# Second attention of a two-layer block: scores per pair of heads, first as rows for the maximum, then with keys on the partitions

## The reference, cut to what matters

```python
q = (x @ Wq).reshape(b, t, 32, 16).transpose(0, 2, 1, 3)
k = (x @ Wk).reshape(b, t, 8, 16).transpose(0, 2, 1, 3)
v = (x @ Wv).reshape(b, t, 8, 16).transpose(0, 2, 1, 3)
q = _apply_rope(q, cos, sin)
k = _apply_rope(k, cos, sin)
k_h = jnp.repeat(k, 4, axis=1)
v_h = jnp.repeat(v, 4, axis=1)
scores = jnp.einsum('bhqd,bhkd->bhqk', q, k_h) / math.sqrt(16)
scores = jnp.where(causal[None, None], jnp.finfo(scores.dtype).min, scores)
attn = jax.nn.softmax(scores, axis=-1)
ctx = jnp.einsum('bhqk,bhkd->bhqd', attn, v_h)
```

## Time and profile before

| | before |
|---|---|
| Three runs, median (lowest to highest) | 1173.53 us (1171.95 to 1173.54) |
| The profiled execution: its own time | 1172.01 us |
| Its span in the trace | 1170.4 us |
| Loop of the second attention, first transposes to last exponentials | 907.6 to 1085.2 us |
| One unit of it (four heads) | 11.03 us |

### The profile page before, as it was taken

How to read it: one execution, slowest core, us unless ns; L and a number is a source line. 1 busy time by engine, 2 the same in 40 slices (tenths; PEclk the granted TensorE clock), 3 DMA queues, 4 the chain that set the end, 5 groups by cost and what they waited for, 6 DMA issues and landing times. The chain is left out here.

```text
span 1170.4 us, 19511 instructions
## 1 busy us (share of the span) xinstructions
PE 1135.4 (97%) x6634; PEld 953.0 (81%) x6634; DVE 787.2 (67%) x2463; ACT 705.8 (60%) x1646; POOL 410.8 (35%) x342
## 2 busy tenths in 40 slices
PE   7999999999999999999999999999999899999997
PEld 5888888888888888888888778888888677777786
DVE  6767776766776777767677752222336899999775
ACT  6656665656765666665665644453112899999524
POOL 4654554354544445544452513334013210020200
PEclk9999999999999999999999999999999999999999
DMA  6011111111110111100100012222001223321001
GB/s 231 19 39 42 39 28 28 28 35 38 46 28 19 37 37 37 36 28 19 37 19 28 1 46 72 63 80 74 1 18 29 56 67 81 99 50 34 1 1 72
DMA packets 30346, 51.04 MB, mean 44 GB/s; under 512 B 5680, under 2 KB 6576, under 8 KB 30256
## 3 DMA queue, kind: packets, MB, share of 16 engines
q1 hardware_dynamic: 29680, 48.85, 14.7%
q10 hardware_dynamic: 576, 1.05, 0.2%
HBM read 38.35 MB, written 2.10 MB: 35 GB/s over the span
## 5 line engine op out<-in xcount | busy, mean ns | idle before, releaser
L491 POOL TENSOR_TENSOR turned<-turned,sin 128x512 f32<-128x512 f32 x73 | 94.6, 1296 | 276.3 <-ACT turned L347 276.3
L363 ACT ACTIVATE probs<-probs,neg_max 128x256 f32<-128x256 f32 (+1 forms) x256 | 119.7, 473 | 11.3 <-DVE neg_max L591 11.3
L1488 ACT ACTIVATE a_probs<-a_probs,a_neg_max 128x512 f32<-128x512 f32 (+3 forms) x256 | 122.6, 562 | 0.1
L1672 DVE CUSTOM_DVE_ANT_0 a_probs<-bank,a_mask 128x512 f32<-128x512 f32 (+3 forms) x256 | 109.8, 485 | 6.0 <-PE bank L1892 6.0
L494 POOL TENSOR_TENSOR turned<-turned,by_cos 128x512 f32<-128x512 f32 x73 | 101.2, 1386 | 11.1 <-DVE by_cos L564 5.7
L96 PE MATMUL bank<-wo_hi,oT_hi 128*128 128x512 f32 x256 | 100.3, 392 | 1.7 <-DVE oT_lo L654 1.7
L745 PE MATMUL bank<-xT_hi,wq_hi 128*128 128x512 f32 x256 | 101.4, 396 | 0.0
L745 PE MATMUL bank<-xT_lo,wq_hi 128*128 128x512 f32 x256 | 100.2, 392 | 0.0
L745 PE MATMUL bank<-xT_hi,wq_lo 128*128 128x512 f32 x256 | 100.1, 391 | 0.0
L96 PE MATMUL bank<-wo_hi,oT_lo 128*128 128x512 f32 x256 | 99.9, 390 | 0.0
L96 PE MATMUL bank<-wo_lo,oT_hi 128*128 128x512 f32 x256 | 99.7, 389 | 0.0
(11 more groups left out here) (234 smaller groups left out, 3155.4 us busy)
## 6 DMA issues: line engine op xcount, KB each, us to landing
staged<-weights SPq DMA_DIRECT2D x70, 256.0 KB, 2.7
f_staged<-weights_f SPq DMA_DIRECT2D x33, 256.0 KB, 2.7
a_q_stack<-a_qT_hi SPq DMA_DIRECT2D x64, 64.0 KB, 2.0
rows<-x_rows SPq DMA_DIRECT2D x2, 1024.0 KB, 7.2
a_k_stack<-a_kT_hi SPq DMA_DIRECT2D x64, 32.0 KB, 2.0
a_q_stack<-a_qT_lo SPq DMA_DIRECT2D x32, 64.0 KB, 2.0
out<-rows SPq DMA_DIRECT2D x8, 256.0 KB, 2.0
a_raw<-weights_qkv SPq DMA_DIRECT2D x4, 384.0 KB, 4.8
```

Source lines behind the costliest of these rows:

```text
L363: act.activation(probs[:, s % 2, h, 0:width], probs[:, s % 2, h, 0:width], ACT.Exp, bias=neg_max[:, s % 2, h:h + 1], scale=SCALE0, accum_o ...
L491: pool.tensor_tensor(at, at, sin[:, :], ALU.mult).then_inc(sin_done, 1)
L1488: act.activation(row_probs(s, qt), row_probs(s, qt), ACT.Exp, bias=neg_max[:, h, qt:qt + 1], scale=-1.0).then_inc(exp_done, 1)
L1672: dve.tensor_tensor_reduce(row_probs(s, qt), ps_s[bank][:, at:at + seen], mask[:, SEQ - seen:SEQ], -SCALE1, HIGHEST, ALU.add, ALU.min, neg ...
```

## The change

The heads are now taken in pairs `p`, 32 of them. For each head the scores are made twice. First as before, queries on the partitions: `scores(p, step)` has three steps, and in each a bf16 matmul of the identity with a causal mask goes ahead of the score matmuls, which add to it. `find_maxima(p, step)` on DVE reduces both heads of the pair in one instruction straight from PSUM and writes only the maxima. `turn_maxima(p)` on PE transposes the eight columns of maxima, `read_maxima(p)` on ACT copies them to SBUF as rows, and `load_maxima(p)` on SP moves them with eight transfers of one row into row 48 of the pair's query stack. `key_scores(p, step)` then makes the scores a second time with the keys on the partitions; key row 48 holds -1, so the maximum is subtracted in the contraction. `exps(p, step)` on ACT reads both heads from PSUM and writes the probabilities in the layout that `apply` wants, so that `turn` and `copy_turned` fall away. `keep_causal(p, step)` on POOL sets the probabilities above the diagonal of the four diagonal blocks to zero. `apply` has three steps, each behind POOL's `kept`.

A stack holds one head with 48 rows, once at partition 0 and once at partition 64 for the pair's other head. `load_stacks(u)` makes 18 transfers of 16 rows, in three buffers; the first three units are loaded ahead of the loop. Scores and key scores share three pairs of banks; the unit's output has one bank in place of two. POOL also sets two pads and two bf16 constants ahead of the loop, and SP loads six rows of -1.

The core of the diff (names and constants that changed alone, and the removed functions, which the listing above shows, are left out):

```diff
-            def load_keys(u, version, arrived):
+            def load_keys(u, arrived):
                 b, g = divmod(u, KV1)
-                for part, source in enumerate((kT_hi, kT_lo, kT_hi)):
-                    to = part * PAIR_ROWS + version * HD1
-                    sp.dma_start(k_stack[to:to + HD1, u % 2, version, :].bitcast(F32),
-                                 source[g * HD1:(g + 1) * HD1, b * SEQ:(b + 1) * SEQ].bitcast(F32)).then_inc(arrived, 16)
+                for at in (0, HALF_ROWS):
+                    for part, source in enumerate((kT_hi, kT_lo, kT_hi)):
+                        to = at + part * HD1
+                        sp.dma_start(k_stack[to:to + HD1, u % BUFFERS, :].bitcast(F32),
+                                     source[g * HD1:(g + 1) * HD1, b * SEQ:(b + 1) * SEQ].bitcast(F32)).then_inc(arrived, 16)
 
             def load_queries(u, pair, arrived):
                 b, g = divmod(u, KV1)
-                first = (g % 2) * GROUP_COLS + pair * PAIR_ROWS
-                for part, source in enumerate((qT_hi, qT_hi, qT_lo)):
-                    sp.dma_start(q_stack[part * PAIR_ROWS:(part + 1) * PAIR_ROWS, u % 2, pair, :].bitcast(F32),
-                                 source[first:first + PAIR_ROWS, g // 2, b * SEQ:(b + 1) * SEQ].bitcast(F32)).then_inc(arrived, 16)
+                for n, at in enumerate((0, HALF_ROWS)):
+                    first = (g % 2) * GROUP_COLS + (2 * pair + n) * HD1
+                    for part, source in enumerate((qT_hi, qT_hi, qT_lo)):
+                        to = at + part * HD1
+                        sp.dma_start(q_stack[to:to + HD1, u % BUFFERS, pair, :].bitcast(F32),
+                                     source[first:first + HD1, g // 2, b * SEQ:(b + 1) * SEQ].bitcast(F32)).then_inc(arrived, 16)
 
             def load_stacks(u):
-                for n in range(2):
-                    arrived = first_stack_in if u == 0 and n == 0 else stack_in[u % 2]
-                    load_keys(u, n, arrived)
-                    load_queries(u, n, arrived)
+                first = first_stack_in if u == 0 else stack_in[u % BUFFERS]
+                load_keys(u, first)
+                load_queries(u, 0, first)
+                load_queries(u, 1, stack_in[u % BUFFERS])
+
+            def load_maxima(p):
+
+                u, pair = divmod(p, 2)
+                sp.wait_ge(max_read, p + 1)
+                for n, at in enumerate((0, HALF_ROWS)):
+                    for qt in range(SEQ_TILES):
+                        row = n * SEQ_TILES + qt
+                        sp.dma_start(q_stack[at + STACK:at + STACK + 1, u % BUFFERS, pair, qt * P:(qt + 1) * P].bitcast(F32),
+                                     max_rows[row:row + 1, p % 2, :].bitcast(F32)).then_inc(max_in[p % 2], 16)
...
+            for n in range(BUFFERS):
+                for at in (0, HALF_ROWS):
+                    sp.dma_start(k_stack[at + STACK:at + STACK + 1, n, :].bitcast(F32), minus[0:1, :]).then_inc(minus_in, 16)
             sp.wait_ge(part_lo, TURNS_OF[0])
...
+            for u in range(BUFFERS):
                 load_stacks(u)
-                if u == 3:
+            for p in range(PAIRS1):
+                load_maxima(p)
+                u = p // 2
+                if p % 2 == 1 and u >= 1 and u + 2 < UNITS1:
+                    if u + 2 == KV1:
+                        sp.wait_ge(part_lo, TURNS_OF[1])
+                    sp.wait_ge(keys_scored, STEPS * (p - 1))
+                    load_stacks(u + 2)
...
+            def read_maxima(p):
+                act.wait_ge(max_turned, p + 1)
+                if p >= 2:
+                    act.wait_ge(max_in[p % 2], MAX_DMAS * (p // 2))
+                act.activation(max_rows[0:2 * SEQ_TILES, p % 2, :], ps_m[0:2 * SEQ_TILES, 0:P], ACT.Copy).then_inc(max_read, 1)
+
+            def exps(p, step):
+
+                act.wait_ge(keys_scored, STEPS * p + step + 1)
+                if step == 0 and p >= RING_PAIRS:
+                    act.wait_ge(applied, STEPS * ((p - RING_PAIRS) // 2 + 1))
+                width, at = STEP_WIDTH[step], step * SEQ
+                act.activation(pair_probs(p)[:, :, at:at + width], ps_pair[KEY_BANKS[step]][:, :, 0:width], ACT.Exp,
+                               scale=SCALE1).then_inc(exp_done, 1)
 
...
+            def keep_causal(p, step):
+
+                pool.wait_ge(exp_done, STEPS * p + step + 1)
+                for kb in KEY_STEPS[step]:
+                    at = step * SEQ + TURNED_AT[kb]
+                    probs = pair_probs(p)[:, :, at:at + P]
+                    last_kept = pool.affine_select(probs, probs, [[0, 2], [1, P]], ALU.is_ge, nothing, base=0,
+                                                   channel_multiplier=-1)
+                last_kept.then_inc(kept, 1)
+
...
+            def find_maxima(p, step):
+
+                if step == 0 and p >= 2:
+                    dve.wait_ge(max_turned, p - 1)
+                by_tile = maxima[:, p % 2, 0:2 * SEQ_TILES].rearrange("p (h t) -> p h t", t=SEQ_TILES)
+                dve.wait_ge(scored, STEPS * p + step + 1)
+                for qt in SCORE_STEPS[step]:
+                    at = SCORES_AT[qt]
+                    found = dve.tensor_reduce(by_tile[:, :, qt:qt + 1], ps_pair[SCORE_BANKS[step]][:, :, at:at + (qt + 1) * P],
+                                              mybir.AxisListType.X, ALU.max)
+                found.then_inc(max_done, 1)
...
+            def scores(p, step):
+
...
+                    elif pair == 0:
+                        pe.wait_ge(stack_in[u % BUFFERS], stacks_loaded(u))
+                if p == 0 and step == 1:
+                    pe.wait_ge(part_lo, PARTS_AFTER[TILES - 2][0] + 1)
+                elif p == 0 and step == 2:
+                    pe.wait_ge(sin_done, 4 * (TILES - 1))
+                elif step == 2 and p >= AHEAD1:
+                    pe.wait_ge(exp_done, STEPS * (p - AHEAD1) + 1)
+                elif p >= AHEAD1 + 1:
+                    pe.wait_ge(exp_done, STEPS * (p - AHEAD1 - 1) + step + 2)
+                elif p >= 1:
+                    pe.wait_ge(max_done, STEPS * (p - 1) + step + 1)
+                banks = ps_pair[SCORE_BANKS[step]]
+                first, end = CAUSAL_AT[step]
+                for n in range(2):
+                    pe.matmul(banks[:, n, first:end], ident_b[:, :], causal_b[:, 0:end - first], start=True, stop=False,
+                              skip_group_check=True)
+                for qt in SCORE_STEPS[step]:
+                    for n, rows_at in enumerate((0, HALF_ROWS)):
+                        part = slice(rows_at, rows_at + STACK)
+                        mm = pe.matmul(banks[:, n, SCORES_AT[qt]:SCORES_AT[qt] + (qt + 1) * P],
+                                       q_stack[part, u % BUFFERS, pair, qt * P:(qt + 1) * P],
+                                       k_stack[part, u % BUFFERS, 0:(qt + 1) * P], start=False, stop=True,
                                        skip_group_check=True)
-                    mm.then_inc(scored, 1)
...
+            def turn_maxima(p):
+                pe.wait_ge(max_done, STEPS * (p + 1))
+                if p == 0:
+                    pe.wait_ge(sin_done, 4 * TILES)
+                else:
+                    pe.wait_ge(max_read, p)
+                pe.transpose(ps_m[:, 0:P], maxima[:, p % 2, :].bitcast(F32), ident[:, :]).then_inc(max_turned, 1)
+
+            def key_scores(p, step):
+
+                u, pair = divmod(p, 2)
+                if step == 0:
+                    if p == 0:
+                        pe.wait_ge(minus_in, 16 * 2 * BUFFERS)
+                    pe.wait_ge(max_in[p % 2], MAX_DMAS * (p // 2 + 1))
+                if step == 0 and p + 1 < PAIRS1:
+                    pe.wait_ge(max_done, STEPS * (p + 2))
+                elif step >= 1 and p + AHEAD1 < PAIRS1:
+                    pe.wait_ge(max_done, STEPS * (p + AHEAD1) + step)
+                else:
+                    pe.wait_ge(exp_done, STEPS * (p - 1) + step + 1)
+                banks = ps_pair[KEY_BANKS[step]]
+                for kb in KEY_STEPS[step]:
+                    for n, rows_at in enumerate((0, HALF_ROWS)):
+                        part = slice(rows_at, rows_at + STACK + 1)
+                        mm = pe.matmul(banks[:, n, TURNED_AT[kb]:TURNED_AT[kb] + SEQ - kb * P],
+                                       k_stack[part, u % BUFFERS, kb * P:(kb + 1) * P],
+                                       q_stack[part, u % BUFFERS, pair, kb * P:SEQ], start=True, stop=True,
+                                       skip_group_check=True)
+                mm.then_inc(keys_scored, 1)
...
+            for p in range(-1, PAIRS1):
+                ahead_too = p + AHEAD1 < PAIRS1
+                if ahead_too:
+                    scores(p + AHEAD1, 0)
+                if p + 1 < PAIRS1:
+                    turn_maxima(p + 1)
+                if p >= 0:
+                    key_scores(p, 0)
+                if p >= 3 and p % 2 == 1:
```

(72 more changed lines are left out.)

252 lines of the change are left out of this document (90 added, 162 removed).

## The result

The changed kernel takes 1350.07 us, the median of 4 runs (1349.66 to 1350.95), against 1172.74 us for the kernel before beside it (4 runs): 1.1513 times as long, with a 95% interval from 1.1493 to 1.1533. The prediction was 1340 us with a range from 1275 to 1380.

What follows compares the result with a forecast made beforehand. Before, PE, ACT and DVE were nearly full together; after, SP's issuing binds: 34 x 0.634 = 21.6 us a unit against PE's 10.3. Projection at 1261 instead of 1093.6, 167 us later, on 1172.0 gives 1339, so 1340 us; range 1275 to 1380.

Steps and rivals of the forecast that it cites:

- One-row issues cost what stacks' do: SP's maxima transfers: taken at the stacks' 0.634 us per issue, with 0.48 to 0.8 us allowed.
- The cheap rival: SP's one-row issues depend on their rows, costing 0.2 to 0.45 us, ending at 1240 to 1295 us; chance 0.13.
- not slower: SP doesn't bind: at 0.25 us an issue PE's 10.3 us sets the pace, 1165 us; threshold 0.32; chance 0.03.
- The start: SP ahead of the loop: issues from 895.2 us, 54 stacks to 929.4, first four pairs of maxima to 952.7.
- The loop: Remaining 13 units: 458 issues at 0.634 us and seven loads to 1247, last four pairs and landing to 1252 us.
- The tail: Last landing to projection: 3.5 us of key scores, exponentials and selections, then 5.5 us; projection at 1261 us.
- the rival on PE's clock: PE idles and its clock falls in the loop, lengthening start, last pairs and tail: 1355 to 1400; chance 0.14 with dearer issues.
- Costs on the compute engines: Work per loop unit after the change: PE 10.3 us, DVE about 8, ACT 6, POOL 3.2 to 5.9.
- PE's longest wait: In the loop: for a transfer of maxima into the query stack, mostly once a unit and some 10 us long.

Runs made afterwards that it cites:

- The run with more work on PE: Changed kernel with 16 more matmuls of 256 bf16 columns on PE behind each pair's last key scores, result unread: 1358.6 us.
- The last version: Changed softmax on the kernel before's 96-row stacks, merged maxima, new order, third maxima buffer, earlier division, some loads on ACT's queue, causal matmuls kept: 1163.0 us, 0.9921 of before.
- The versions with 14 issues a unit and fewer: Changed softmax on the kernel before's 96-row stacks, maxima merged: 1180.6 us; without causal matmuls 1176.9; three more edits 1164.35; key transfers on ACT 1154.98; causal matmuls back 1163.0.

## Why the prediction was right, point by point

- **One-row issues cost what stacks' do.** The one price that no row showed: 0.589 us long and 0.63 us apart in the trace, 0.61 where they were doubled or taken away. The cheap rival (0.2 to 0.45 us) falls, and so does *not slower*, which needed under 0.32.
- **The start.** First issue predicted at 895.2, measured 895.09; the 54 stacks until 929.4, measured 929.2; the four first pairs until 952.7, measured 953.4.
- **The loop is undersized by 6 us.** Its last landing was to come at 1252 us; the chain of waits of the changed kernel has

```profile
1255.78 0.59 SPq L1467
1256.41 3.40 DMA a_q_stack<-a_max_rows
1259.82 0.04 issue
```

  that is 1259.8. From 953.4 to 1257.0 us the loop took 303.6 us against 1250 - 952.7 = 297.3: some issues are dearer than the median (up to 1.77 us for a stack's), and the gapless stretch of 24 that gave 0.634 us had none of these. Of the other 1.5 us, 0.7 are the later start (953.4 for 952.7) and 0.8 the landing, 2.8 us behind the end of the last issue in place of 2.0.
- **The tail is undersized by 3 us.** From that landing to the projection at 1271.7 it took 11.9 us; I had 9. In these 14 us PE is busy 10.4 at a clock of 0.75:

```profile
1257.00:1271.00 14.00, 10.40 (x81) 4.96 (x74) 3.36 (x7) 4.42 (x7) 2.86 (x8) 0.75 0.01 2
```

  The run with more work on PE shows what this clock costs. There the same way runs at full clock, and its chain from the last landing to the projection has

```profile
1267.69 1.94 DMA a_q_stack<-a_max_rows
...
1271.34 1.85 PE banks L2066 x16
...
1280.50 2.75 PE banks L96 x12
```

```profile
1269.60:1280.50 10.90, 9.16 (x89) 5.98 (x90) 3.94 (x8) 4.11 (x6) 1.68 (x5) 1.00 0.01 2
```

  that is 10.9 us, of which 1.85 are added matmuls (L2066): 9.0 without them, as predicted. This is what is true of the rival on PE's clock: the clock did fall in the loop, SP covered it there, and it shows at the end. With the 7.8 us above, the 2.9 make the projection 10.7 us later than predicted, and the time is 10 us above 1340.
- **Costs on the compute engines held**: DVE 7.6 us a unit (8 predicted), ACT 5.8 (6), POOL 3.2 without its other work (3.2 to 5.9). PE's 10.3 can't be compared at the lower clock, but it counted the two heads' scores one after the other, and they ran side by side (last section), so it was too high; with SP as the bound this made no difference.
- **PE's longest wait was named wrong.** I had it for the maxima, about 10 us once a unit. PE waits 62.6 us for stacks and 42.5 for maxima, 8 us a unit together. `scores` of the next unit stand ahead of `key_scores` in PE's queue, and their stacks ahead of the maxima in SP's. For the time it made no difference, as one queue feeds both; once the issues were merged, it was the next bound (38.6 us).

The cause is shown from three sides: the issues added to the kernel before (1339.5), doubled (+155.6), and taken away (-137). The last version, with the changed softmax, few issues, the circles opened and loads on ACT's queue, is 0.8% faster than the kernel before; how much of that is the softmax alone is not shown, as the kernel before was not given the other edits.

## What to carry to other kernels

Count the issues of each queue for a unit of the loop, at the price of the same kind of transfer in the trace, as you count an engine's work: here 34 small transfers at 0.63 us outweighed what DVE (10.34 to 7.6 us a unit) and ACT (10.46 to 5.8) had been relieved of. Merge transfers before moving them to another queue, since there they stand in line with that engine's work. And when one bound is lifted, look for the circle behind it (who is ahead of whom in two queues), which costs next to nothing until then.

## What was not expected of the hardware

- The two heads' scores, 48 rows at partitions 0 and 64, ran side by side, which the prediction left open. On PE in the changed kernel, before the loop and at full clock:

```profile
904.30 0.49 PE L1955 MATMUL banks<-a_k_stack,a_q_stack 48*128 48x512 f32 x2
904.72 0.50 PE L96 MATMUL banks<-a_w_hi,a_xT 128*128 128x512 f32 x1
```

  In the last version, with 96 rows from partition 0 for either head:

```profile
960.02 0.71 PE L1963 MATMUL banks<-a_k_stack,a_q_stack 96*128 96x512 f32 x2
960.63 0.33 PE L1975 MATMUL banks<-identity,a_maxima 128*128 128x128 f32 x1
```

  The two of 48 rows are over in 0.49 us, as long as one matmul of 128 rows (0.50), where the two of 96 rows take 0.71. "TensorEngine Tiling (Array Packing)" of the Trainium skill (Tiling Modes, Key Properties) says that tiles of 64 rows run in parallel; the trace agrees for these. From the first of the two to the next matmul it is 0.42 us, against 0.61 with 96 rows. The versions with 14 issues a unit and fewer gave the stacks of 48 rows up, so what they would be worth there is open.
- PE's granted clock rose when it was given work that nothing reads: in the same 21.5 us of the loop from 0.66 with 86 matmuls to 0.82 with 114.
- A transfer of eight rows of 512 bytes into two rows of 2 KB costs about the same issue as one of one row: median 0.54 us into partitions 48 and 112, 0.66 us into 96 and 97, in place of 0.59.
